# The first pass of a Macaron block: turns, units and the Dskip product in another order

## What is computed

```python
x = x + 0.5 * ffn(layernorm(x))          # weights rounded to -1, 0, 1 times a scale, plus a bias
x = x + mamba(layernorm(x))
x = x + 0.5 * ffn(layernorm(x))          # the same weights
# mamba:
xz = x @ W_in.T;  u, z = split(xz)
u = silu(conv_b + causal convolution of u over 4 tokens, per feature)
x_dbl = u @ W_xproj.T                     # 64 + 16 + 16 columns: dt_r, B, C
dt = softplus(dt_r @ W_dt.T + b_dt)
h = exp(dt * A) * h + dt * B * u          # 16 states a feature, over all tokens
y = sum_n h * C + u * Dskip
out = (y * silu(z)) @ W_out.T
```

## Time and profile before

| | |
|---|---|
| median of three runs | 3207.58 us |
| profiled execution, its own time | 3209.26 us |
| its span | 3207.4 us |
| first pass | about 1100 us of the span |
| DVE busy, in the pass of the change / after it | 5 to 7 tenths of a slice / 9 tenths |
| granted TensorE clock, mean | 0.887 of full speed |

### The profile page before, as it was taken

One profiled execution on the slowest core, in us unless ns is written; L12 is line 12 of the kernel. 1 busy time (PEld: TensorE's weight loads), 2 busy tenths in 40 slices (PEclk: granted clock), 3 DMA queues, 4 the chain that ended last, 5 costly groups with the idle time before them and its releaser, 6 DMA issues.

```text
span 3207.4 us, 41798 instructions
## 1 busy us (share of the span) xinstructions
PE 2488.6 (78%) x12320; PEld 1435.1 (45%) x12320; DVE 2755.0 (86%) x3590; ACT 1748.9 (55%) x3158; POOL 1774.5 (55%) x1497
## 2 busy tenths in 40 slices
PE   3578888988988357788878777778787777788787
PEld 1233434434433145554555444545545445455453
DVE  6565776776775499999999999999999999999993
ACT  2334676575676555555555555555555555555552
POOL 1111222222221177777777777787777877777773
PEclk8789999999988677998889889899898988898989
DMA  6543322323332442122122121221221221212101
GB/s 216 206 156 130 127 93 100 126 100 107 111 116 77 148 175 70 47 80 70 56 85 72 42 75 62 75 71 59 81 71 54 72 73 54 70 60 79 43 27 40
DMA packets 152830, 286.68 MB, mean 89 GB/s; under 512 B 40128, under 2 KB 89536, under 8 KB 148224
## 3 DMA queue, kind: packets, MB, share of 16 engines
q1 hardware_dynamic: 152576, 283.71, 26.0%
HBM read 174.09 MB, written 109.58 MB: 88 GB/s over the span
## 4 chain that ended last, share of the span: by engine, by line
POOL 26%; issue 21%; DVE 16%; PE 1%; POOLq 1%; ACT 0%; DMA 0%; DVEq 0%; SPq 0%
POOL dbu L1009 19%; DVE h L1177 9%; DVE y L1187 5%; POOL x L1033 2%; POOL o L1039 1%; POOL y L1029 1%; POOL dbu L1014 1%; POOL carry L1020 1%; PE p_g L1312 1%; POOLq L40 1%; DVE tokt L1209 1%; PE p_g L1302 0%; POOL small L69 0%; DVE q L1200 0%; DVE x L1220 0%
## 5 line engine op out<-in xcount | busy, mean ns | idle before, releaser
L1096 ACT ACTIVATE p_da<-dt,neg_a 128x255 f32<-128x255 f32 x2048 | 891.5, 468 | 870.0 <-DVE h L1177 869.7
L1177 DVE TENSOR_TENSOR_SCAN h<-p_da,dbu 128x512 f32<-128x512 f32 x1024 | 1192.8, 1207 | 19.7 <-POOL dbu L1014 15.5
L1009 POOL TENSOR_TENSOR dbu<-dtu,bb 128x1024 f32<-128x1024 f32 x512 | 1197.1, 2360 | 0.8 <-issue 0.2
L1279 PE MATMUL p_ht<-ident,h 128*128 128x128 f32 x4096 | 644.3, 318 | 340.9 <-DVE h L1177 338.4
L1279 PEld LDWEIGHTS p_ht<-ident,h 128*128 128x128 f32 x4096 | 561.1, 165 | 449.8 <-issue 266.1
L1187 DVE SCALAR_TENSOR_TENSOR y<-p_ht,ct,y 128x1024 f32<-128x1024 f32 x512 | 646.6, 1263 | 0.0
L1312 PE MATMUL p_g<-wo,tokt 128*128 128x512 f16 x1536 | 362.4, 395 | 3.3 <-DVE tokt L1209 3.3
L1321 PE MATMUL p_g<-wz,xz 128*128 128x512 f16 x1536 | 351.2, 386 | 0.0
L706 PE MATMUL p_u<-xz,wu 128*128 128x512 f16 x1536 | 350.3, 385 | 0.0
L358 POOL TENSOR_TENSOR late<-dt,u 128x512 f32<-128x512 f32 x64 | 82.4, 1287 | 425.4 <-DVE dt L550 425.4
L697 PE MATMUL p_ffn<-tern,xt 128*128 128x512 f16 x1024 | 258.2, 416 | 63.0 <-DVE xt L500 62.9
(11 more groups left out here) (112 smaller groups left out, 2754.3 us busy)
## 6 DMA issues: line engine op xcount, KB each, us to landing
bb<-b_scratch SPq DMA_DIRECT2D x128, 256.0 KB, 3.3
xin<-in_x SPq DMA_DIRECT2D x32, 512.0 KB, 4.4
x_scratch<-x SPq DMA_DIRECT2D x32, 512.0 KB, 3.3
xz_scratch<-xz SPq DMA_DIRECT2D x16, 1024.0 KB, 5.5
y_scratch<-late SPq DMA_DIRECT2D x32, 512.0 KB, 2.9
dt_scratch<-dt SPq DMA_DIRECT2D x64, 256.0 KB, 2.2
dtu_scratch<-late SPq DMA_DIRECT2D x64, 256.0 KB, 2.5
dt<-dt_scratch SPq DMA_DIRECT2D x16, 1024.0 KB, 6.4
```

The costliest lines, as they stand in the source:

```text
L1009: nc.gpsimd.tensor_tensor(state[:, 4 * f:4 * f + 4, :], dtu[par][:, 4 * f:4 * f + 4, :], bb[n // NB % 2][:, n % NB:n % NB + 1, :].to_broad ...
L1096: ins_ = nc.scalar.activation(p_da[p % 2][:, k * T2 + 1:(k + 1) * T2], dt[par][:, g, 1:], ACT.Exp, scale=neg_a[:, g, n:n + 1])
L1177: nc.vector.tensor_tensor_scan(h[n % 2][:, 2 * p:2 * p + 2, :].rearrange("p g t -> p (g t)"), p_da[p % 2][:], dbu[n % 2][:, 2 * p:2 * p + ...
L1279: mm = nc.tensor.transpose(p_ht[t][:, g * P:(g + 1) * P], h[n % 2][:, g, t * P:(t + 1) * P], ident[:])
```

## The change

Seven things change. (1) `turn(1, k)` moves to the start of step k+1, ahead of `ffn(k+1)`, and `turn(0, k+1)` moves into step k, between the two u-products; the first turn is done in the prologue. Each turn has semaphores of its own. (2) All s phases move behind the FFN on PE. (3) Odd feature groups of u are evacuated, convolved and passed through silu in their own step, not in the next. (4) y units turn u itself, and DVE multiplies by Dskip, broadcast over partitions, as it takes the bank out; `times_dskip` and `ud` are gone. Dskip is loaded as 128x1024 (512 KB), not as 128x8. (5) Order and phases of the units change a little. (6) The weight items (`w_work`, `w_high`) move on DVE behind the FFN addition and the statistics of x1, and on ACT behind `normalise(1, k)`. On POOL all dt * u of a step stand behind the second `row_scale`; the place of L351, ahead of that `row_scale`, is the same. (7) The store of xz moves to the start of the next block, ahead of the store of x1 and the load of x.

```diff
+units = [("y", 0), ("x", 0), ("y", 1), ("c", 0), ("d", 0), ("y", 2), ("d", 1), ("y", 3), ("d", 2), ("d", 3),
+         ("y", 4), ("d", 4), ("y", 5), ("d", 5), ("y", 6), ("d", 6), ("d", 7), ("y", 7)]
...
+def turned(k, f_on):
+    if isinstance(k, int):
+        return 0 < k <= L // P
+    return f_on
...
 # SP, step: after the stores of phases 0 and 1 and the weight transfers
+if j == 0 and turned(k, f_on):
+    for b in range(2):
+        wait_alone(sp, tr_split[1][b], k)
+    for a in range(2):
+        sp.dma_start(dram["xz"][...], xz[par][:, a]...)
 if f_on:
     (store of x1 row k, load of x row k + 2)
...
 # ACT, step
+if turned(k, f_on):
+    (at j = 1: wait for u_full and xz_stored)
+    high(1, k - 1, ...) for both banks
+if f_on and not last(k):
+    normalise(0, xin[(j + 1) % 2][:], k + 1)
+s_work(i - 1, j, 0)
+normalise(1, x1[j % 2][:], k)
+w_high(i, j)
+u_work(i, 2 * j)
+s_work(i - 1, j, 1)
+high(0, k + 1, ...) for both banks
+silu(i, par, 2 * j)
+s_work(i - 1, j, 2)
+u_work(i, 2 * j + 1)
+s_work(i - 1, j, 3)
+silu(i, par, 2 * j + 1)
...
 # DVE, a y unit
-nc.vector.tensor_copy(y0[...], p_s[v % 2][:]...)
-if g + 2 < G:
-    times_dskip(d, dpar, g + 2)
+nc.vector.tensor_tensor(y0[...], p_s[v % 2][:]..., dskip[:, g * P:(g + 1) * P]...to_broadcast(...), ALU.mult)
 # DVE, step
+(wait for x row k + 1) row_stats(xin ..., k + 1)
+low(1, k - 1, ...) for both banks
 FFN addition and row_stats(x1 ..., k)
+s_work(d, 1 - par, j, 0)
+w_work(i, j)
+conv(i, 2 * j)
+s_work(d, 1 - par, j, 1)
+low(0, k + 1, ...) for both banks
+s_work(d, 1 - par, j, 2)
+conv(i, 2 * j + 1)
+s_work(d, 1 - par, j, 3)
...
 # PE, step
+turn(1, k - 1)
 ffn(k)
+s_work(i - 1, 1 - par, j, 0)
 u_product(i, par, 2 * j)
+s_work(i - 1, 1 - par, j, 1)
+turn(0, k + 1)
 u_product(i, par, 2 * j + 1)
+s_work(i - 1, 1 - par, j, 2)
+s_work(i - 1, 1 - par, j, 3)
```

More of the change, by code:

```diff
@@ L444, in prologue @@
                                              ).then_inc(tern_done, 1)
+                    for b in range(2):
+                        high(0, 0, xt[:, 0, 4 * b:4 * b + 4, :], b)
                 def w_high(i, j):
@@ L457, in step @@
                 def step(i, par, j, f_on, u_on, s_on):
[L458 to L482, removed]
+                    k = (i + 1) * TT1 + j
+                    if turned(k, f_on):
+                        f, jj, into = (i + 1, j - 1, xz[1 - par]) if j else (i, TT1 - 1, xz[par])
+                        if jj == 0:
                             wait(act, u_full, (f - 1) * G)
@@ L594, in prologue @@
                     dve.wait_ge(const_loaded, 16 * 7)
+                    for b in range(2):
+                        low(0, 0, xt[:, 0, 4 * b:4 * b + 4, :], xt[:, 1, 4 * b:4 * b + 4, :], b)
                 def factor(m):
@@ L634, in step @@
                     k = f * TT1 + j
-                    if f_on:
-                        for b in range(2):
[L637 to L643, removed]
-                        conv(i if j else i - 1, (2 * j - 1) % G)
-                    w_work(i, j)
-                    if s_on:
-                        s_work(d, 1 - par, j, 0)
-                        s_work(d, 1 - par, j, 1)
+                    if f_on and not last(k):
+                        wait(dve, x_loaded[(j + 1) % 2], (f * 2 + (j + 1) // 2 + 1) * 16)
+                        row_stats(dve, nc, xin[(j + 1) % 2], stats[0], mv[0], vn[0], small[:, 40:41], ln_chain[0],
+                                  stats_ready[0], scale_ready[0], k + 1)
+                    if turned(k, f_on):
+                        jj, into = (j - 1, xz[1 - par]) if j else (TT1 - 1, xz[par])
+                        for b in range(2):
+                            hi, lo = (into[:, a, jj // 2, 4 * b:4 * b + 4, (jj % 2) * P:(jj % 2 + 1) * P] for a in range(2))
+                            low(1, k - 1, hi, lo, b)
                     if f_on:
@@ L669, in step @@
                     if s_on:
+                        s_work(d, 1 - par, j, 1)
+                    if f_on and not last(k):
+                        for b in range(2):
+                            low(0, k + 1, xt[:, 0, 4 * b:4 * b + 4, :], xt[:, 1, 4 * b:4 * b + 4, :], b)
+                    if s_on:
+                        s_work(d, 1 - par, j, 2)
+                    if u_on:
+                        conv(i, 2 * j + 1)
+                    if s_on:
                         s_work(d, 1 - par, j, 3)
-                    if u_on and j == TT1 - 1:
-                        times_dskip(i, par, 0)
-                        times_dskip(i, par, 1)
                 drive(dve, step, prologue)
@@ L681, in turn @@
                     for b in range(2):
[L682 removed]
+                        if n:
+                            if not last(k):
+                                wait(pe, tr_split[0][b], k + 2)
+                        else:
+                            wait(pe, tr_split[1][b], k - 1)
                         for q in range(4):
```

113 lines of the change are left out of this document (50 added, 63 removed).

## The result

The changed kernel takes 3256.82 us (median; 3255.97 to 3257.87) beside 3207.75 for the kernel before on the same chip: a ratio of 1.0153 with an interval of 1.0135 to 1.0171. The forecast of 3215 had the sign right, but the time is 42 us above it and outside the range. The profiled execution took 3256.53 us with a span of 3254.7, which is 47.3 more than the span before.

A forecast was written before the change was run, and what follows sets the result against it. Three early stretches decide: A by ACT, DVE, POOL and weight items, B by nearly full PE, C by ACT's dt chain. 3209.3 - 22.6 + 32.2 - 3 = 3215.9, less 1.7 is 3214.2, stated as 3215; range 3185 to 3237 us.

The forecast's parts named there:

- The failed step: Block start to d1 at j = 1: PE is the bound, nothing stops it; 27.9 us for j = 0, together 50.
- The walk: One block followed through all four engines from PE's turn(1) at j = 0; it gave 112.3 us a block.
- B: Blocks 1 to 6, 265.28 to 955.37 us, PE nearly full; 690.1 us was to fall to 667.5, 22.6 saved.
- stretch C: Blocks 7 and 8, a chain of dt units on ACT; 3 us saved, bounds 10 and -3.
- Stretch A: Steps k = 0 to 7, first to ninth FFN; 229.1 us was to become 260.7, 31.6 lost.
- The 0.6 for the constants: Start of the kernel: the larger Dskip load may delay the first FFN by 0.6 us.
- the list: Forecast lengths of steps k = 0 to 7, built from x loads, weight items and POOL's gaps; sum 260.7 us.
- What it said would show: Signs: ninth FFN near 297 us, DVE x waits, blocks of 112 us with low(0) waits, no normalised-row waits in blocks 1 to 6.
- The load of x behind xz: Block start j = 0: load lands at 34 to 35.5, d0 starts 0.4 to 2 us later, covered by ACT's 2.7 slack.
- It doesn't do what it says in B: Rival, 0.14: ACT and POOL hold blocks at 116 us, only A and C count; 3237 us.
- The rival of faster blocks: Rival, 0.16: j = 2 and 3 chain closes earlier, PE sets blocks at 98 to 105 us; 3140 to 3180 us.
- The upper bound of a block of 119: Blocks 1 to 6: handovers at 0.2 us and half clock for one more FFN give 119 us a block, 17 lost.

The follow-up runs named there:

- the wait filled: In the changed kernel, PE does the x unit ahead of the first u-product at each block start; 3215.88 us, ratio 1.0019.
- the split early: In the changed kernel, high and low of turn 1 of a block's last row move to the end of step j = 3; 3220.19 us, ratio 1.0033.
- The two experiments on them: Each against the changed kernel: POOL's all-reduce put behind row_scale of x1, 3236.49 us; x load issued ahead of the weight transfers in the first 8 steps, 3239.36 us.
- the last version: Changed kernel plus early weight items, early x unit, POOL's addition moved, x load ahead of weights, late all-reduce at k = 3, x load ahead of xz store; 3140.82 us.
- POOL's addition moved: Changed kernel with early weight items and early x unit, plus POOL's bias/2 addition for row k+1 put ahead of step k's dt * u; 3154.31 us, ratio 0.9825.
- part 4 alone: Kernel before with only u turned by PE and the Dskip product taken from PSUM by DVE, order otherwise as before; 3200.69 us, ratio 0.997.

## Why the prediction was wrong

- **The failed step** is the sentence "From turn(1) at j = 0 to the d1 product at j = 1 PE is the bound and nothing stops it", and its 27.9 us for j = 0. The walk took turn(1), FFN, y0 and u-product in a row. It held the split of the last row as early "as the change wants", but that holds only for a row with a step between its turn and its use. The last row of a block is turned at j = 0 and used by the first u-product of the same j = 0, behind a DVE that still has convolution, y7, d7 and statistics in front. In five blocks of B PE waited 34.2 us for it, in block 7 another 11.2. The runs with the wait filled or shortened show that it was on the path in B.
- **The price of that step.** B was to be 667.5 us and is 696.2, 28.7 more; with the wait filled it is 658.9, with the split early 663.2. From its FFN to the next one, step j = 0 took 36.1 to 37.5 us in the five blocks, against 27.9 in the walk; with the wait filled it took 28.6 to 29.5.
- **The second term that failed** is stretch C, "3 us saved", by "the same walk". It lost 8.0, 11 more than forecast. The wait of 11.2 us in block 7 doesn't account for it by itself: without it C is only 3.4 us shorter. The cause of the other 7.6 us stays open. What PE then still waits for in C are the last silu of block 6 (7.6), DVE's emptying of a bank (6.94) and the silu ahead of the x unit of block 8 (7.10, before 3.05).
- **A match that is luck.** With only the wait filled the kernel takes 3215.88 us, and the forecast was 3215. But B is then 8.6 us below its forecast and C 7.6 above: two errors cancel.
- **The block.** Walked: 112.3. Measured: 118.0 (five blocks from 313.52 to 903.66), 110.6 with the wait filled and 111.5 with the split early. So the rest of the walk, fillers for handovers and clock included, was 1 to 2 us too long. With the wait filled B is 31 us shorter than in the kernel before; which of parts 1, 2, 3 and 5 bring that, no run separates.
- **Stretch A was right.** Predicted 31.6; measured 33.8. The 0.6 for the constants was 0.16 (the first FFN at 36.37 in place of 36.21). The steps k = 0 to 7 took 20.5, 37.0, 28.3, 38.1, 32.9, 34.7, 38.7 and 32.6 us, against 20.9, 39.1, 27.3, 37.2, 33.1, 32.5, 38.0 and 32.6 in the list. POOL's gaps of 8.59 and 10.88 us and the waits for x are there. The two experiments on them return 20 and 17.5 us. But the 33.8 is a difference: the place of the items costs 50 and the rest brings 16.
- **What it said would show.** The ninth FFN near 297 us: 299.23. Waits for x in the steps 1 to 7: 47.7 us in 6. PE waiting for low(0) at block starts: 2.11 us at 643.92. Waits for normalised rows gone from B: 17.3 before, 2.4 after. All of it came, and the blocks of 112 did not.
- **Dskip.** 684 ns as the copy; right. That it frees "only the wait at the block's start" fits: alone it took 14.1 us of such waits away and gained 9.
- **The load of x behind xz** was priced at nothing behind ACT's slack. It landed after 7.7 us at most block starts, sooner than the 9 to 10.5 of the walk, and in the last version its place cost some 4 us over six blocks.
- **The rivals.** "It doesn't do what it says in B" was nearest: 3237, with a B of 690.1. It had the right stretch but the wrong place (ACT and POOL), and B was 6.0 us above even that, with C 11 above. The rival of faster blocks named the right place for what was left, `row_scale` behind POOL's addition: only with that moved did a block come below its 109.7, to 107.7. The range ended at 3237 because no case in it had a wait of PE that was new. The upper bound of a block of 119 was in the text, and 17 lost in B would have made 3255: I worked out that bound and then did not carry it into the range.

## What to carry to other kernels

When a step is moved across a loop edge, list for each buffer who reads it and how far behind the new place, in the first and in the last iteration too: three rows had a step of slack and the fourth had none, and filling that one wait brought 41 us. What runs on the side, here the weight items, goes where the engines wait anyway, and not between a result and its next reader; the same items cost 50 us from one place to the other. The sum of a wait is no price for its removal, in either direction: the x load gave back 17.5 of 47.7 us in one version and 12 of 14.6 in another, and the early split took 29.5 us off PE's waits and 36.6 off the time. And when a total agrees with a forecast, compare its parts: here two errors of 8 us hid behind it.

## What the runs showed of the hardware

- A `partition_all_reduce` costs POOL on both sides: where the idle time is put down to issue, it is 5.70 to 6.91 us ahead of it and 6.79 to 11.59 us behind it over all versions, for an operation of 0.41 us. The prediction knew the second side alone. Put late in step 3 it gained nothing, since step 4 lost what step 3 gained.
- Blocks 2 to 5 are two passes of a loop, two blocks a pass. At the start of the second pass, and at no other block start above 1.9 us, DVE stood 2.38 to 2.67 us with nothing that the profile shows to wait for, in every version of the changed kernel (2.58 at 658.71, above; 2.40 with POOL's addition moved, below). In six versions PE stood there too, 2.20 to 3.64 us (2.92 with POOL's addition moved). There the block that ends behind it was 111.1 us long, its neighbours 107.7. In the kernel before no such idle time is seen there, but with part 4 alone DVE stood 3.23 us (606.86). What the engines do in it, no run shows.

```profile
574.11 1.96 PE L688 MATMUL p_tr<-ident,xn 128*128 128x128 f32 x8 [2.92 <-issue]
...
586.95 1.29 DVE L54 BATCH_NORM_STATS2 small<-xin 128x6 f32<-128x512 f32 x2 [2.40 <-issue]
```
